# Counts of neighbours at 3.2 instead of 2.67 windows a lot, compared in pairs, and a first dense phase of three batches

## The chip, the cores and the metric

The kernel runs on one core of one Trainium2 chip. The metric is the device time of one execution in microseconds.

## The reference

Two graph layers over 6250 nodes of 256 features and 206250 edges (`src`, `dst`, sorted by `dst`; one of 8 types each), cut to what matters:

```
h  = relu(layernorm(x))
x1 = x + segment_sum(einsum('ni,roi->rno', h, weight)[edge_type, src], dst) + bias0
h  = relu(layernorm(x1))
deg = number of edges with dst n (and 1 for the node itself); dinv = 1/sqrt(deg)
out = x1 + leaky_relu(segment_sum(dinv[src]*dinv[dst] * (h @ W)[src], dst) + b, 0.2)
```

## The kernel before

Nodes are held in 50 tiles of 128. The program first normalises `x` into a table, checks the edge list and prepares keys; then `both_layers` does both layers at once. Its work is ordered by slots `n` = 0 to 578, which every engine runs through in its own loop; `Plan` computes, ahead of time, what falls into which slot.

**First layer, the lots.** Slot n below 539 has a lot: 384 edges (3 chunks of 128). POOL gathers the source rows of each chunk (L1099, 3 gathers a lot) into a ring of `RING0` = 7 lots. ScalarE makes the lot's one-hot matrices (`build_gap` L1338, three instructions, and `build_onehot` L1346), four slots ahead. TensorE sums the lot (`sum_lot`, L1599, 6 matmuls), which frees the ring's place; VectorE adds the sums to `acc` (`accumulate`, L1416), two lots at a time, since two lots share a PSUM bank and two banks are used. Every 11 lots are one tile's step: TensorE projects it with the 8 weights in two parts (`project`, L1615), VectorE and ScalarE finish and normalise it (`stage_a`, `stage_b`, `stage_c`), SyncE stores it to `table1` (L1128).

**Second layer, the counts.** The second layer is a dense product with a matrix of counts (how many edges lead from node j to node i). It is made window by window, 800 windows of 8 target nodes: VectorE compares the window's keys with node numbers (`build_hot`: L1492 for `hot_m`, 4 x 100 columns, and L1495 for `hot_lo`, 4 x 128), TensorE multiplies the two one-hots (`count`, L1629, 4 matmuls, into one of `NCOUNT` = 3 PSUM banks), ScalarE evacuates them (`evacuate`, L1275) and stores them to `counts_d`. `hots` holds `NHOT` = 8 windows; a window is counted `LEAD` = 3 slots behind its comparison. The keys of 128 windows are one set; for each of the 7 sets POOL looks up records (`look` L1080, `fetch` L1087), VectorE finds offsets and keys (`offsets` L1457 and L1459, `window_keys`), TensorE turns them (L1639), SyncE carries degrees out and in (L1196, L1203). These have slots in `Plan` that lie a fixed number ahead of the slot in which the set is first needed, `due`.

**Second layer, the dense product.** A unit is one group of 4 target tiles (13 groups) by one batch of source tiles (12 batches, `BATCHES`, mostly 5 tiles). It has two halves, each one piece in a slot: 2 matmuls of 512 columns for each source tile (`dense`, L1659; one tile of one half is called a half tile in this text). ScalarE widens the unit's counts (`widen`, L1331), SyncE loads them (`load_counts`, L1155) and the batch's features (`load_stash`, L1139), VectorE adds each piece to its sums (`add_dense`, L1523 for the first, L1525). While counting goes on, only one PSUM bank serves pieces, and there is at most one piece in two slots. First come the units of the first `EARLY_GROUPS` = 6 groups with the first `FIRST_BATCHES` = 4 batches; then SyncE moves their sums to HBM (`move_away`, L1160, 3 MB), and the other groups' units follow in the same place; when counting ends, the sums come back (`move_back`). `Plan` models TensorE's load with a pace of 3.85 us a slot and fills in pieces where there is room. A batch can't be used before its last tile is stored: batch 3 (the fourth) is there from slot 238.

The plan that results: windows in slots 13 to 312 in the rhythm 3, 3, 2, counted in slots 16 to 315; `counts_end` = 320; the move away at slot 263; 156 units, of which 1184 half tiles before lot 539 and 116 after. Half tiles per 20 slots, from slot 60 to 579: 20, 10, 0, 40, 30, 20, 45, 15, 5, 50, 35, 45, 45, 85, 80, 85, 80, 85, 80, 65, 85, 74, 65, 40, 95, 21. At the end `project1` (L1678), `close` (L1535, L1540) and POOL's addition (L1106) finish the tiles.

## Time and profile before

| | us |
|---|---|
| median of 3 runs | 2302.07 |
| lowest, highest | 2300.12, 2308.04 |
| the profiled execution, its own time | 2306.06 |
| its span, first to last instruction | 2304.3 |
| TensorE's mean granted clock | 0.953 |
| busy: TensorE, VectorE, ScalarE, POOL | 2007.3, 1219.7, 1608.9, 1643.0 |

The rows name PE for TensorE, PEld for its weight loads, DVE for VectorE, ACT for ScalarE, SP for SyncE. An idle time is put down to what ended it; "issue" means that the profile shows nothing that was waited for.

### The profile page before, as it was taken

How to read it: one execution, taken by the hardware profiler on the slowest of the kernel's cores; microseconds unless marked ns; L12 is line 12 of the kernel's file. 1: busy time of each engine (PE TensorE's matmuls, PEld its weight loads, DVE VectorE, ACT ScalarE, POOL GpSimd, SP SyncE). 2: the span in 40 equal slices, each digit the busy share in tenths (PEclk: the TensorE clock that was granted, in tenths of full speed). 3: DMA queues.
4: the chain of work that ended last, by engine and by line, in shares of the span. 5: the costliest groups of instructions: out<-in, count | busy, mean ns of one | idle time of the engine just before them, and what ended most of it. 6: DMA issues, size and time to landing. Idle time of an engine off the chain costs nothing.

```text
span 2304.3 us, 44662 instructions
## 1 busy us (share of the span) xinstructions
PE 2007.3 (87%) x14354; PEld 1797.4 (78%) x14354; DVE 1219.7 (53%) x3510; ACT 1608.9 (70%) x3919; POOL 1643.0 (71%) x1740
## 2 busy tenths in 40 slices
PE   1567788887888898879899899999999999999897
PEld 1456777776787887768788889898888898989676
DVE  7446567667568666766656633323223232334267
ACT  4646677786878888678777877776767777676440
POOL 5577777777777777777766777777777777777414
PEclk9698999999999999999989999999999999999999
DMA  9446567656766776667776777765766666666485
GB/s 289 121 123 189 177 200 225 210 186 201 244 218 222 252 232 203 187 218 241 233 246 197 238 256 243 228 194 170 222 200 190 191 196 191 183 190 162 105 225 168
DMA packets 353088, 470.37 MB, mean 204 GB/s; under 512 B 113158, under 2 KB 264886, under 8 KB 352726
## 3 DMA queue, kind: packets, MB, share of 16 engines
q0 software_dynamic: 79072, 216.18, 31.9%
q1 hardware_dynamic: 228246, 165.07, 24.5%
q10 hardware_dynamic: 45536, 86.22, 10.2%
q8 instruction: 119, 1.95, 0.4%
q14 instruction: 115, 0.94, 0.1%
HBM read 348.61 MB, written 118.71 MB: 203 GB/s over the span
## 4 chain that ended last, share of the span: by engine, by line
PE 60%; POOL 13%; issue 7%; ACT 7%; DMA 5%; DVE 4%; ACTq 1%; DVEq 0%; POOLq 0%; SPq 0%
PE ps_slot L1599 21%; PE ps_slot L1659 13%; PE ps_proj L1615 13%; POOL rows_f L1099 12%; PE ps_aux L1659 9%; DMA rows_f<-table,idxT 3%; PE ps_slot L1629 3%; ACT gap_f L1338 2%; ACT staging_f L1275 2%; ACT wide_f L1331 1%; DMA abuf_f<-counts_d 1%; DVE hots_f L1495 1%; DVE hots_f L1492 1%; ACT onehot_f L1346 1%; ACT acc_f L1261 1%
## 5 line engine op out<-in xcount | busy, mean ns | idle before, releaser
L1099 POOL DMA_INDIRECT rows_f<-table,idxT x1617 | 1538.2, 951 | 510.3 <-issue 473.8
L1599 PE MATMUL ps_slot<-onehot_f,rows_f 128*128 128x128 f32 x6468 | 870.4, 287 | 150.7 <-DMA rows_f<-table,idxT 121.8
L1599 PEld LDWEIGHTS ps_slot<-onehot_f,rows_f 128*128 128x128 f32 x6468 | 824.8, 200 | 184.3 <-DMA rows_f<-table,idxT 134.7
L1338 ACT ACTIVATE gap_f<-iota,keyT 128x128 bf16<-128x128 bf16 x1617 | 528.6, 394 | 81.1 <-ACT staging_f L1275 49.6
L1275 ACT ACTIVATE staging_f<-ps_slot 128x400 bf16<-128x400 f32 x800 | 345.8, 500 | 182.2 <-PE ps_slot L1629 179.2
L1492 DVE TENSOR_TENSOR hots_f<-ps_slot,keys_f 128x400 bf16<-128x400 bf16 x800 | 285.2, 357 | 303.5 <-PE ps_slot L1629 299.5
L1615 PE MATMUL ps_proj<-w0t,acc_f 128*128 128x256 f32 x1600 | 375.8, 389 | 0.0
L1659 PE MATMUL ps_slot<-wide_f,stash_f 128*128 128x512 f32 (+1 forms) x1410 | 345.2, 390 | 1.6 <-ACT wide_f L1331 1.5
L1346 ACT ACTIVATE onehot_f<-gap_f 128x384 f32<-128x384 bf16 x539 | 277.5, 515 | 96.6 <-PE ps_slot L1599 96.4
L1416 DVE TENSOR_TENSOR acc_f<-ps_slot,acc_f 128x256 f32 x539 | 227.2, 422 | 219.5 <-PE ps_slot L1599 151.3
L1615 PEld LDWEIGHTS ps_proj<-w0t,acc_f 128*128 128x128 f32 x1600 | 303.2, 195 | 45.4 <-issue 1.6
L1495 DVE TENSOR_TENSOR hots_f<-ps_slot,keys_f 128x512 bf16<-128x512 bf16 x800 | 329.6, 412 | 0.0
L1659 PE MATMUL ps_aux<-wide_f,stash_f 128*128 128x512 f32 x1190 | 308.4, 404 | 3.0 <-ACT wide_f L1331 3.0
L1659 PEld LDWEIGHTS ps_slot<-wide_f,stash_f 128*128 128x128 f32 x1410 | 248.0, 190 | 45.1 <-ACT wide_f L1331 2.5
L1331 ACT ACTIVATE wide_f<-abuf_f 128x512 fp32r<-128x512 bf16 (+1 forms) x404 | 217.5, 608 | 84.0 <-PE ps_slot L1659 52.0
L1629 PE MATMUL ps_slot<-hots_f 128*128 128x100 bf16 x3200 | 217.0, 211 | 60.9 <-ACT staging_f L1275 44.9
L1629 PEld LDWEIGHTS ps_slot<-hots_f 128*128 128x128 bf16 x3200 | 193.6, 115 | 87.3 <-issue 48.1
L1659 PEld LDWEIGHTS ps_aux<-wide_f,stash_f 128*128 128x128 f32 x1190 | 218.4, 193 | 44.4 <-issue 3.4
L1331 ACT ACTIVATE wide_f<-keys_f 128x512 fp32r<-128x512 bf16 (+1 forms) x215 | 117.0, 598 | 62.5 <-PE ps_slot L1659 52.9
L1525 DVE TENSOR_TENSOR sums_e_f<-ps_slot,sums_e_f 128x512 f32<-128x512 f32 x88 | 60.9, 692 | 162.7 <-PE ps_slot L1659 162.5
L1106 POOL TENSOR_TENSOR acc_f<-acc_f 128x256 f32<-128x256 f32 x50 | 36.6, 732 | 93.9 <-DVE acc_f L1540 90.9
L1261 ACT ACTIVATE acc_f<-ident 128x2048 f32<-128x2048 f32 x52 | 99.6, 1915 | 0.0
(156 smaller groups left out, 871.5 us busy)
## 6 DMA issues: line engine op xcount, KB each, us to landing
abuf_f<-counts_d SPq DMA_DIRECT2D x66, 640.0 KB
rows_f<-table,idxT POOLq DMA_INDIRECT x1617
stash_f<-table SPq DMA_DIRECT2D x15, 1280.0 KB, 7.7
keys_f<-counts_d SPq DMA_DIRECT2D x30, 640.0 KB
table<-hs_f SPq DMA_DIRECT2D x50, 256.0 KB
table<-xres SPq DMA_DIRECT2D x10, 640.0 KB, 6.7
acc_f<-x_d SPq DMA_DIRECT2D x50, 128.0 KB, 2.7
x_d<-xt_f SPq DMA_DIRECT2D x49, 128.0 KB
```

The costliest lines, as they stand in the source:

```text
L1099: eng.indirect_dma_start(rows0[:, k, c, :], None, V["table0"], bass.IndirectOffsetOnAxis(ap=idxT[:, n * LOT + c:n * LOT + c + 1], axis=0)) ...
L1275: eng.activation(staging[:, h % 2, :, (w % HSUB) * SUB:(w % HSUB + 1) * SUB], count_bank(w)[:, 0:SPAN * MW].rearrange("p (d t) -> p t d", ...
L1331: eng.activation(wide_of(i, u).rearrange("p (h c) -> p h c", c=HW), counts, ACT.Copy).then_inc(s_wide, 1)
L1338: last = eng.activation(gap[:, n % 2, c, :], iota[:, :], ACT.Abs, scale=-1.0, bias=V["key"][:, n * LOT + c:n * LOT + c + 1])
L1346: eng.activation(onehot[:, n % HOTS, :, :], gap[:, n % 2, :, :], ACT.Relu, scale=-1.0, bias=1.0).then_inc(s_oh, 1)
L1416: eng.tensor_tensor(win, part, win, ALU.add).then_inc(s_acc, 1)
L1492: eng.tensor_tensor(hot_m[:, w % NHOT, :, :].rearrange("p s (m q) -> p s m q", q=2), m_numbers.rearrange("p (m q) -> p m q", q=2).unsqueez ...
L1495: eng.tensor_tensor(hot_lo[:, w % NHOT, :, :], lo_numbers, lo_e[:, b % 2, k, :].unsqueeze(1).to_broadcast([P, P, SPAN]), ALU.is_equal).the ...
L1599: last = eng.matmul(o[:, b * W:(b + 1) * W], rows0[:, k, c, b * P:(b + 1) * P], onehot[:, n % HOTS, c, :], start=(c == 0), stop=(c == LOT ...
L1615: last = eng.matmul(ps_proj[:, 0:DF], acc[:, b * R + r, a:a + P], V["w0t"][:, r, b, :], start=False, stop=(r == R - 1 and b == NB - 1))
L1629: last = eng.matmul(o[:, j * MW:(j + 1) * MW], hot_lo[:, w % NHOT, :, j], hot_m[:, w % NHOT, j, :], start=True, stop=True)
L1659: last = eng.matmul(o, stash[:, k % 2, t, p * DF + half * P:p * DF + (half + 1) * P].bitcast(f32r), wide_of(w, u), start=(t == 0 and p == ...
```

## The change

Three things change together. `build_hots` compares two windows with one instruction of 800 and one of 1024 elements (`hot_m` and `hot_lo` of two neighbouring windows), so `s_hot` rises by one per pair, and waits until the places of both in `hots` are free. The windows are spread over 5/16 x 800 = 250 instead of 300 slots, in the rhythm 4, 4, 2, 4, 2, and the key work's distances to `due` are cut by 8 slots or 5. And `FIRST_BATCHES` is 3. The one-hots of the lots are made as before, all by ScalarE.

```diff
--- before.py
+++ after.py
@@ -16,7 +16,7 @@
 GROUP = 4
 EARLY_GROUPS = 6
 STAGED_GROUPS = 3
-FIRST_BATCHES = 4
+FIRST_BATCHES = 3
 MOVE_SLOTS = 5
 BATCH = 5
 BATCHES = (5, 5, 5, 5, 5, 5, 5, 5, 3, 2, 2, 3)
@@ -696,25 +696,26 @@
     def __init__(self, D):
         self.nlot = D.segs * LOTS
         self.tail = self.nlot + SEAM
-        last_window = D.nsub * 3 // 8
+        last_window = D.nsub * 5 // 16
         self.counts_end = FIRST_WIN + last_window + LEAD + 4
         self.win = {}
-        for w in range(D.nsub):
-            self.win.setdefault(FIRST_WIN + w * last_window // D.nsub, []).append(w)
+        assert D.nsub % 2 == 0 and NHOT % 2 == 0
+        for w in range(0, D.nsub, 2):
+            self.win.setdefault(FIRST_WIN + w * last_window // D.nsub, []).extend((w, w + 1))
         counted = [FIRST_WIN + (end * D.nw - 1) * last_window // D.nsub + LEAD + 9 for _, end in D.group]
         self.look, self.fetch, self.count_at, self.key_at, self.turn_at = {}, {}, {}, {}, {}
         self.degree_out, self.degree_in = {}, {}
         for b in range(D.sets):
             due = FIRST_WIN + b * P * last_window // D.nsub
-            self.look[due - 44 if b else 0] = b
+            self.look[due - 36 if b else 0] = b
             for i in range(len(PARTS)):
-                self.count_at[(due - 42 if b else 0) + i] = (b, i)
-            self.degree_out[due - 38 if b else 4] = b
-            self.degree_in[due - 36 if b else 6] = b
-            self.fetch[due - 30 if b else 5] = b
+                self.count_at[(due - 34 if b else 0) + i] = (b, i)
+            self.degree_out[due - 30 if b else 4] = b
+            self.degree_in[due - 28 if b else 6] = b
+            self.fetch[due - 22 if b else 5] = b
             for i in range(2):
-                self.key_at[(due - 18 if b else 8) + i] = (b, i)
-            self.turn_at[due - 14 if b else 10] = b
+                self.key_at[(due - 13 if b else 8) + i] = (b, i)
+            self.turn_at[due - 9 if b else 10] = b
         self.turn_win = {}
         for n, b in self.turn_at.items():
             self.turn_win[b] = min(w for m, ws in self.win.items() if m + LEAD > n for w in ws)
@@ -1278,7 +1279,7 @@
             def copy_keys(b):
 
                 if b >= 2:
-                    eng.wait_ge(s_hot, P * (b - 1))
+                    eng.wait_ge(s_hot, P // 2 * (b - 1))
                 eng.wait_ge(s_tp, b + 1)
                 keys, lows = (turned(b)[:, i * SPAN * P:(i + 1) * SPAN * P].rearrange("p (s w) -> p s w", s=SPAN) for i in range(2))
                 eng.activation(key_e[:, b % 2, :, :, :].rearrange("p w s q -> p s w q"),
@@ -1481,19 +1482,20 @@
                     eng.scalar_tensor_tensor(lo_w[:, :, :], hi_i[:, :, :], -float(P), rec2[:, :, :, 1], ALU.mult, ALU.add).then_inc(s_kw, 1)
                     eng.tensor_tensor(key_w[:, :, :], key_w[:, :, :], hi_i[:, :, :], ALU.add).then_inc(s_kw, 1)
 
-            def build_hot(w):
+            def build_hots(w):
 
                 b, k = divmod(w, P)
+                a = w % NHOT
                 eng.wait_ge(s_ke, 2 * (b + 1))
                 if w >= NHOT:
-                    eng.wait_ge(s_cnt, w - NHOT + 1)
+                    eng.wait_ge(s_cnt, w - NHOT + 2)
                 if w == 0:
                     eng.wait_ge(s_np, 1)
-                eng.tensor_tensor(hot_m[:, w % NHOT, :, :].rearrange("p s (m q) -> p s m q", q=2),
-                                  m_numbers.rearrange("p (m q) -> p m q", q=2).unsqueeze(1).to_broadcast([P, SPAN, MW // 2, 2]),
-                                  key_e[:, b % 2, k, :, :].unsqueeze(2).to_broadcast([P, SPAN, MW // 2, 2]), ALU.is_equal)
-                eng.tensor_tensor(hot_lo[:, w % NHOT, :, :], lo_numbers,
-                                  lo_e[:, b % 2, k, :].unsqueeze(1).to_broadcast([P, P, SPAN]), ALU.is_equal).then_inc(s_hot, 1)
+                eng.tensor_tensor(hot_m[:, a:a + 2, :, :].rearrange("p a s (m q) -> p (a s) m q", q=2),
+                                  m_numbers.rearrange("p (m q) -> p m q", q=2).unsqueeze(1).to_broadcast([P, 2 * SPAN, MW // 2, 2]),
+                                  key_e[:, b % 2, k:k + 2, :, :].rearrange("p w s q -> p (w s) q").unsqueeze(2).to_broadcast([P, 2 * SPAN, MW // 2, 2]), ALU.is_equal)
+                eng.tensor_tensor(hot_lo[:, a:a + 2, :, :], lo_numbers.unsqueeze(1).to_broadcast([P, 2, P, SPAN]),
+                                  lo_e[:, b % 2, k:k + 2, :].unsqueeze(2).to_broadcast([P, 2, P, SPAN]), ALU.is_equal).then_inc(s_hot, 1)
 
             def add_own(h):
 
@@ -1579,8 +1581,8 @@
                     offsets(*PL.count_at[n])
                 if n in PL.key_at:
                     window_keys(*PL.key_at[n])
-                for w in PL.win.get(n, ()):
-                    build_hot(w)
+                for w in PL.win.get(n, ())[::2]:
+                    build_hots(w)
                 for k in PL.fin.get(n - 1, ()):
                     close(k)
 
@@ -1619,7 +1621,7 @@
 
             def count(w):
 
-                eng.wait_ge(s_hot, w + 1)
+                eng.wait_ge(s_hot, w // 2 + 1)
                 if w >= NCOUNT:
                     eng.wait_ge(s_ev, w - NCOUNT + 1)
                 if w in turn_of:
```

The plan that results: windows compared in slots 13 to 262 and counted in slots 16 to 265; `counts_end` = 270; the first phase has 18 units instead of 24, and the move away comes at slot 210; `stash` is loaded 17 times instead of 19. Half tiles per 20 slots, from slot 60: 20, 10, 10, 35, 45, 0, 40, 35, 40, 50, 65, 85, 80, 80, 80, 85, 20, 75, 55, 10, 85, 74, 65, 40, 95, 21; 1184 before lot 539 and 116 after. Units begin at slots 183, 187, 191, 196, 200, 206, 215, 219, 223, 228, 232, 237, 242, 246, 251, 255, 259, 264 and so on.

TensorE in slots 215 to 219. L1599 is a lot, L1629 the counts (4 matmuls a window), L1615 a projection. Before:

```order
L1599 MATMUL ps_slot<-onehot_f,rows_f 128x128 x6
L1629 MATMUL ps_slot<-hots_f 128x100 x12
L1599 MATMUL ps_slot<-onehot_f,rows_f 128x128 x6
L1615 MATMUL ps_proj<-w0t,acc_f 128x256 x8
L1629 MATMUL ps_slot<-hots_f 128x100 x8
L1599 MATMUL ps_slot<-onehot_f,rows_f 128x128 x6
L1629 MATMUL ps_slot<-hots_f 128x100 x12
L1599 MATMUL ps_slot<-onehot_f,rows_f 128x128 x6
L1629 MATMUL ps_slot<-hots_f 128x100 x12
L1599 MATMUL ps_slot<-onehot_f,rows_f 128x128 x6
L1629 MATMUL ps_slot<-hots_f 128x100 x8
```

The same slots in the changed kernel, where the lines are L1601, L1631, L1617, and L1661 is a dense piece:

```order
L1601 MATMUL ps_slot<-onehot_f,rows_f 128x128 x6
L1631 MATMUL ps_slot<-hots_f 128x100 x8
L1661 MATMUL ps_aux<-wide_f,stash_f 128x512 x10
L1601 MATMUL ps_slot<-onehot_f,rows_f 128x128 x6
L1617 MATMUL ps_proj<-w0t,acc_f 128x256 x8
L1631 MATMUL ps_slot<-hots_f 128x100 x16
L1601 MATMUL ps_slot<-onehot_f,rows_f 128x128 x6
L1631 MATMUL ps_slot<-hots_f 128x100 x16
L1661 MATMUL ps_aux<-wide_f,stash_f 128x512 x10
L1601 MATMUL ps_slot<-onehot_f,rows_f 128x128 x6
L1631 MATMUL ps_slot<-hots_f 128x100 x8
L1601 MATMUL ps_slot<-onehot_f,rows_f 128x128 x6
```

The counts of a slot went from 8 or 12 matmuls to 8 or 16, and a dense piece stands in every second slot where there was none.

VectorE about slot 219 to 220, before: an addition of a lot to `acc`, the last stage of a tile (L1442), `own` (L1504) and the comparisons of four windows.

```order
L1416 ISA
L1416 TENSOR_TENSOR acc_f<-ps_slot,acc_f 128x16x16
L1442 TENSOR_TENSOR hs_f<-hs_f 128x256
L1504 TENSOR_TENSOR own_f<-staging_f,identb 128x64
L1492 TENSOR_TENSOR hots_f<-ps_slot,keys_f 128x400
L1495 TENSOR_TENSOR hots_f<-ps_slot,keys_f 128x512
L1492 TENSOR_TENSOR hots_f<-ps_slot,keys_f 128x400
L1495 TENSOR_TENSOR hots_f<-ps_slot,keys_f 128x512
L1492 TENSOR_TENSOR hots_f<-ps_slot,keys_f 128x400
L1495 TENSOR_TENSOR hots_f<-ps_slot,keys_f 128x512
L1492 TENSOR_TENSOR hots_f<-ps_slot,keys_f 128x400
L1495 TENSOR_TENSOR hots_f<-ps_slot,keys_f 128x512
```

In the changed kernel, with a burst of key offsets (L1458, L1460), the lines L1494 and L1497 comparing pairs:

```order
L1460 TENSOR_REDUCE n_less_f<-keys_f 128x1
L1458 TENSOR_SCALAR keys_f<-recs_f,startp 128x512
L1460 TENSOR_REDUCE n_less_f<-keys_f 128x1
L1494 TENSOR_TENSOR hots_f<-ps_slot,keys_f 128x800
L1497 TENSOR_TENSOR hots_f<-ps_slot,keys_f 128x1024
L1494 TENSOR_TENSOR hots_f<-ps_slot,keys_f 128x800
L1497 TENSOR_TENSOR hots_f<-ps_slot,keys_f 128x1024
L1396 TENSOR_LOAD offr
L1417 ISA
L1417 TENSOR_TENSOR acc_f<-ps_slot,acc_f 128x16x16
L1417 ISA
```

Four windows took eight comparisons, of 400 and 512 columns; four now take four, of 800 and 1024. The offsets of set 6, which came at slots 259 to 262, now stand here.

## Rows read from the trace of the kernel before

**Rows 1.** The page, busy us of each engine, share of the span, instructions.

```profile
PE 2007.3 (87%) x14354; PEld 1797.4 (78%) x14354; DVE 1219.7 (53%) x3510; ACT 1608.9 (70%) x3919; POOL 1643.0 (71%) x1740
```

**Rows 2.** Line L1099, the gathers: durations ns, first and last start; POOL's idle time before them.

```profile
L1099 POOL DMA_INDIRECT rows_f<-table,idxT x1617: 942/949/1781, 75.8 to 2165.8; - x180
...
  issue: 473.8, 1554
  PE ps_slot L1599: 36.5, 63
```

**Rows 3.** Waits of POOL from 1120 to 1350 us: total us, times, longest.

```profile
POOL rows_f L1099 <- PE ps_slot L1599: 20.1, 10, 4.7
```

**Rows 4.** Gathers (L1099) by stretch: us, POOL busy (count), clock, DMA share, GB/s.

```profile
70.00:810.00 740.00, 533.36 (x560) 0.92 0.63 197
70.00:1170.00 1100.00, 796.93 (x836) 0.93 0.65 205
70.00:1340.00 1270.00, 912.64 (x958) 0.93 0.66 207
1410.00:1820.00 410.00, 310.30 (x328) 1.00 0.68 199
```

**Rows 5.** Additions to acc (L1416) by stretch, VectorE busy (count).

```profile
70.00:810.00 740.00, 76.29 (x182) 0.92 0.63 197
70.00:1170.00 1100.00, 113.12 (x270) 0.93 0.65 205
70.00:1340.00 1270.00, 130.72 (x312) 0.93 0.66 207
810.00:920.00 110.00, 12.13 (x29) 0.97 0.68 214
```

**Rows 6.** All engines by stretch: PE, PEld, DVE, ACT, POOL busy (count).

```profile
1170.00:1340.00 170.00, 155.04 (x1236) 139.31 (x1235) 107.25 (x338) 136.54 (x337) 115.72 (x123) 0.96 0.70 223
1410.00:1820.00 410.00, 410.00 (x2509) 366.70 (x2508) 123.78 (x296) 295.49 (x700) 310.30 (x328) 1.00 0.68 199
```

**Rows 7.** Waits from 1170 to 1340 us.

```profile
DVE hots_f L1492 <- PE ps_slot L1629: 42.4, 19, 5.6
...
ACT staging_f L1275 <- PE ps_slot L1629: 20.9, 16, 3.2
...
PE ps_slot L1629 <- ACT staging_f L1275: 10.7, 6, 3.8
```

**Rows 8.** Timeline of TensorE: start us, us, instruction (a lot's 6 matmuls appear as 12).

```profile
1104.32 0.70 PE L1629 MATMUL ps_slot<-hots_f 128*128 128x100 bf16 x12
1104.86 1.57 PE L1599 MATMUL ps_slot<-onehot_f,rows_f 128*128 128x128 f32 x12
```

**Rows 9.** Timeline of VectorE, comparisons.

```profile
1199.43 0.35 DVE L1492 TENSOR_TENSOR hots_f<-ps_slot,keys_f 128x400 bf16<-128x400 bf16 x1
1199.70 0.41 DVE L1495 TENSOR_TENSOR hots_f<-ps_slot,keys_f 128x512 bf16<-128x512 bf16 x1
1200.03 0.35 DVE L1492 TENSOR_TENSOR hots_f<-ps_slot,keys_f 128x400 bf16<-128x400 bf16 x1
```

**Rows 10.** The page, evacuation of counts: busy us, mean ns, idle before.

```profile
L1275 ACT ACTIVATE staging_f<-ps_slot 128x400 bf16<-128x400 f32 x800 | 345.8, 500 | 182.2 <-PE ps_slot L1629 179.2
```

**Rows 11.** Timeline of VectorE and TensorE behind a burst of key offsets.

```profile
1129.71 0.41 DVE L1416 TENSOR_TENSOR acc_f<-ps_slot,acc_f 128x256 f32 x1
...
1130.91 0.55 PE L1599 MATMUL ps_slot<-onehot_f,rows_f 128*128 128x128 f32 x1 [6.34 <-DVE acc_f L1416]
```

**Rows 12.** The page, fp32 additions from PSUM, 256 and 512 columns: busy us, mean ns.

```profile
L1416 DVE TENSOR_TENSOR acc_f<-ps_slot,acc_f 128x256 f32 x539 | 227.2, 422 | 219.5 <-PE ps_slot L1599 151.3
...
L1525 DVE TENSOR_TENSOR sums_e_f<-ps_slot,sums_e_f 128x512 f32<-128x512 f32 x88 | 60.9, 692 | 162.7 <-PE ps_slot L1659 162.5
```

**Rows 13.** Waits of the whole span before counting matmuls.

```profile
PE ps_slot L1629 <- ACT staging_f L1275: 44.9, 37, 4.1
...
PEld ps_slot L1629 <- DVE hots_f L1495: 25.5, 34, 2.7
```

## Prediction

> **What bounds the kernel now.** I read the page's busy shares first, then the gathers' own line, then the stretches. TensorE is busy for 87% of the span and POOL for 71% [rows 1], which points to TensorE, but the gathers say otherwise: a gather occupies POOL for 0.949 us and the next begins 0.305 us later (473.8 us of "issue" gaps over 1554 times), a step of 1.254 us. There are 1617 gathers and 35 look-ups of the same length, and 1652 x 1.254 = 2072 us; they run from 75.8 to 2166.8 us, 2091 us [rows 2]. So for 91% of the span the kernel goes at the pace at which POOL can issue: 3 gathers, 3.76 us a lot. POOL lost only 2091 - 2072 = 19 us to anything else. The line lists 63 waits for TensorE's L1599, 36.5 us; 10 of them, 20.1 us, lie between 1120 and 1350 us [rows 3], and the other 53 average 0.31 us, the ordinary gap. Taking the ordinary gap off, the stall in that one stretch is 20.1 - 3 = **17 us**, and it is all that a change of TensorE's, VectorE's or ScalarE's work before lot 539 can win.
>
> Why it is there: the ring holds 7 lots. The gathers issued up to a time, divided by 3, less the lots added to `acc` by then, are the lead of POOL in lots (those landed and summed but not yet added included). Up to 810 us it is 560/3 - 182 = 4.7. By 1170 us it is 836/3 - 270 = 8.7, and by 1340 us 958/3 - 312 = 7.3, with POOL waiting in between: the ring is full [rows 4, 5]. From 1170 to 1340 us, 42 lots take 170 us, 4.05 us each; TensorE is busy 155.0 us of them (3.69 a lot), ScalarE 136.5 (3.25), VectorE 107.3 (2.55) [rows 5, 6]. These are lots 270 to 311, where counting (2.67 windows a lot) and the dense pieces of phase two run together. Afterwards TensorE is busy 410 us of 410, but POOL issues 328 gathers in them, 411 us' worth: TensorE just keeps up [rows 4, 6]. Behind the last gather come 137 us of tail.
>
> **The change, part by part.**
>
> *Two windows per comparison.* The comparison of 400 elements begins 0.27 us before that of 512, which begins 0.33 us before the next: 0.60 us a window [rows 9]. 112 more elements cost about 0.055 us, 0.49 ns each, which leaves some 0.075 us per instruction. A pair then costs 800 x 0.49 + 0.075 = 0.47 and 1024 x 0.49 + 0.075 = 0.58 us, 1.05 against 1.20: over 400 pairs VectorE has about 60 us less to do. It is not the last to arrive in the full stretch (it waits 42.4 us for TensorE's counts in 170 us [rows 7]), so I cost this at nothing; were VectorE full, 3.2 x 0.075 = 0.24 us a lot would come back. Per lot VectorE's comparisons go from 2.67 x 0.60 = 1.60 to 3.2 x 0.525 = 1.68 us.
> The 400 elements come from PSUM and go through in 0.27 us, 1.5 elements a nanosecond. The Trainium skill (VectorE: DVE Perf Modes, the perf-mode tier table) gives two-tensor operations with any PSUM operand one element per cycle at 0.96 GHz. This trace speaks against that; by that rule a pair would be near 2 us, and that is a rival below.
>
> *3.2 windows a lot.* TensorE: three windows take 1104.86 - 1104.32 = 0.54 us, 0.18 each; 0.53 more a lot is **0.10 us a lot** [rows 8]. ScalarE: an evacuation keeps it busy 345.8/800 = 0.43 us, so 0.23 us a lot more, 3.25 to 3.48 of 3.76 us [rows 6, 10]. The slots now hold 4, 4, 2, 4, 2 windows, before 3, 3, 2. There are three count banks, so a fourth window in a slot must wait until the first has been evacuated: one evacuation lasts 0.50 us [rows 10], TensorE is there 0.54 us after it began the first, so the wait is at least some 0.2 us when ScalarE is prompt. When it isn't, the nearest rows are the waits that exist: 10.7 us in 6 times, 1.8 us each [rows 7]. Three slots in five: between 0.12 and 1.1 us a lot. I take 0.2, near the lower end, because ScalarE itself stood waiting for counts 16 times in these 42 lots [rows 7], so it is often there first.
> Eight windows of one-hots are kept. Before, 8 windows were exactly three slots' work, so VectorE, building for slot n, needed the counts of TensorE's slot n. 3.2 x 3 is 9.6, so now it needs part of slot n + 1, and what stands behind the comparison on VectorE (the additions of the lots, the addition of a dense piece, both with TensorE waiting for them) comes up to a slot later. Bound from below nothing (TensorE has a slot in between); from above the one case in the trace: VectorE's burst of key offsets, at the end of which TensorE had stood 6.34 us for L1416 [rows 11]. Six such bursts remain; I take nothing for those before lot 183, where POOL's lead is short and covers them, and 0.1 us a lot in the full stretch for this.
>
> *Counting ends at lot 267 instead of 317; phase one is 3 batches (18 units), moved away at slot 210 instead of 263.* Dense work before lot 539 and after it is unchanged (1184 and 116 half tiles), and from slot 458 on both plans are the same, so **the tail costs the same**. Gathers and look-ups keep their number; on POOL look-ups 1 to 6 move to earlier lots. SyncE issues the 3 MB moves earlier and two `stash` loads fewer. What changes is where the dense work lies. While counting goes on, the old plan has pieces of 240 half tiles in slots 180 to 320, with nearly nothing between 206 and 238. The new one has them from 183 to 210 and without a break from 215 to the end of counting (the order of TensorE in slots 215 to 219, shown above, is where it begins; 11 units of 5 halves x 2 in 52 slots, 2.2 half tiles a lot; the old full stretch: 10 units in slots 268 to 311, 2.3). So the mixture that filled the ring for 42 lots now comes for 52, with denser counts, and it comes straight after 27 lots of the same kind.
>
> **The sum.** Full stretch: 4.05 (as now) + 0.10 (counts) + 0.2 (fourth window) + 0.1 (VectorE later) = 4.45; less 0.1 since the clock in my reference was 0.96 and the burst of offsets no longer coincides with the move: **4.35 us a lot** against POOL's 3.76. 52 lots x 0.59 = 31 us. Lots 183 to 210 now run at 110/29 = 3.79 [rows 5, 6]; with 0.3 more, 27 x 0.33 = 9 us of lead are used. The lead at 810 us, 4.7 lots, leaves 8.7 - 4.7 = 4 lots or 15 us to fill, and slots 210 to 215 give back 3 us: 15 - 9 + 3 = 9, of which I count 7, since the lead wanders by a lot. Stall 31 - 7 = 24 us, and 1 us for going into the dense stretch, where TensorE has no spare, with a full ring. Gone is the old stall of 17. Net 24 + 1 - 17 = **+8 us**: 2306.06 becomes 2314 for the profiled run, and, as that run lies 4 us above the median of the runs, 2302.07 becomes **2310 us**. Ends: with 4.1 us a lot the stall is 18 - 9 = 9 us, net -8; with 4.65 it is 46 - 7 = 39 and up to 5 us more later, net +27.
>
> **The rivals.**
> *The stall goes (faster).* The old stall began when a burst of key offsets on VectorE, the move of 3 MB and the first load of counts behind it fell into slots 259 to 268; TensorE stood 6.34 us at its start [rows 11], and the lead went from short to full within 120 us. Now the move (210) and the burst (219 to 222) are nine slots apart and VectorE has spare time. If TensorE then holds 3.9 us a lot, 52 x 0.14 = 7 us fit into the lead and the stall is gone: 2302 - 17 = 2285; half gone, 2293. It decides at about 4.2 us a lot (52 x 0.44 = 23, less 9, is 14: a gain of 3). Against it: from 1170 to 1340 us, long after the burst, the pace stayed at 4.05.
> *Nothing changes.* The stall moves 50 lots earlier with its size: 2302, within 7 us. A measurement of this kernel can tell about 0.3%, 7 us, from no change.
> *Paired comparisons fall to one element a cycle.* The fp32 additions from PSUM go one by one: 512 elements take 0.27 us more than 256, 1.05 ns each [rows 12]. If the pair's shapes lose the rate that the 400-element rows show and fall to this one, a pair takes 1824 x 1.05 = 1.92 us and twice 0.075, 2.07; 1.6 pairs a lot are 3.3 us, and VectorE's other work in the full stretch is 2.55 - 1.60 = 0.95: 4.25 us a lot through all 250 lots of counting, 0.49 x 250 = 120 us less the lead: about 2410. The tier table of the Trainium skill (VectorE: DVE Perf Modes) would have it so. The rows for 400 elements, with the same operand in PSUM, do not [rows 9].
> *A pair comes too late.* A count now waits for both windows' comparisons. TensorE's weight loads waited for L1495 34 times [rows 13]; at 0.5 us more each, 17 us over 250 lots, of which a third falls where it counts: +5 us on the forecast's side. The Trainium skill (Perfetto Trace Analysis, Optimizing Scalar/DVE Operations) advises breaking instructions up where an engine that isn't full makes others wait, which speaks against pairing.
>
> **How the numbers follow.** Forecast, stall larger (late pairs included): 0.50, of which 0.11 within 0.3%. Nothing changes: 0.15, with 0.01 to either side. Stall mostly or wholly gone: 0.32, of which 0.29 over 0.3%. One element a cycle: 0.03. Together faster 0.30, same 0.27, slower 0.43. The range takes in half to nearly all of the gain and the upper end of the sum: 2288 to 2330.
>
> **What would show it.** In the profile after: POOL's waits for L1599 over 0.5 us at about lots 220 to 270 (900 to 1100 us), 24 us of them; a pace of 4.35 us a lot there; L1494 and L1497 at a step of 0.47 and 0.58 us; TensorE's L1631 waiting for ScalarE far more often than the 37 times of now [rows 13]; the last gather at about 2175 us and again 137 us behind it. I am wrong if POOL's waits for TensorE fall below 17 us in all, or if the last gather comes before 2160 us, or if the tail changes by more than 3 us.

## The result, and the profile after

| | before | after |
|---|---|---|
| median, us (4 runs of each, on one chip) | 2301.10 | 2455.95 |
| lowest, highest | 2299.66, 2308.04 | 2452.55, 2463.31 |
| profiled execution: own time, span | 2306.06, 2304.3 | 2452.55, 2450.3 |
| TensorE's mean granted clock | 0.953 | 0.940 |

The ratio is 1.0671, with a 95% interval from 1.0652 to 1.069: slower by 155 us where 8 were forecast, and far above the range. The direction was right, the size was not.

The page of the kernel after, busy us of each engine, beside [rows 1]; then the gathers, the evacuations and the two paired comparisons (busy, mean ns | idle before them):

```profile
PE 2037.2 (83%) x14354; PEld 1823.9 (74%) x14354; DVE 1171.3 (48%) x2710; ACT 1615.8 (66%) x3919; POOL 1639.0 (67%) x1740
...
L1100 POOL DMA_INDIRECT rows_f<-table,idxT x1617 | 1533.8, 949 | 658.9 <-issue 454.0
...
L1276 ACT ACTIVATE staging_f<-ps_slot 128x400 bf16<-128x400 f32 x800 | 340.1, 502 | 206.5 <-PE ps_slot L1631 201.7
...
L1494 DVE TENSOR_TENSOR hots_f<-ps_slot,keys_f 128x800 bf16<-128x800 bf16 x400 | 228.0, 570 | 388.7 <-PE ps_slot L1631 387.5
...
L1497 DVE TENSOR_TENSOR hots_f<-ps_slot,keys_f 128x1024 bf16<-128x1024 bf16 x400 | 271.8, 680 | 0.0
```

Hardly any engine has more to do: POOL 4 us less, VectorE 48 less, ScalarE 7 more, and TensorE 30 more, at a mean granted clock of 0.940 instead of 0.953. All shares have fallen. So the 146 us by which the span grew are, nearly all, waiting. The gathers tell whose. The same line by itself: durations, first and last start, POOL's idle time before them:

```profile
L1100 POOL DMA_INDIRECT rows_f<-table,idxT x1617: 940/946/1265, 75.4 to 2309.4; - x180
...
  issue: 454.0, 1490
  PE ps_slot L1601: 204.9, 127
```

The last gather starts at 2309.4 instead of 2165.8 us [rows 2]: 143.6 us later; behind it come 140.9 us instead of 138.5. POOL waited 204.9 us for TensorE's lot sums instead of 36.5, and its ordinary gaps shrank by 19.8: 148.6 us more of standing, the whole loss. When? Gathers and additions by stretch, beside [rows 4, 5] (us, POOL or VectorE busy with them (count), clock, DMA share, GB/s):

```profile
70.00:400.00 330.00, 232.68 (x245) 0.85 0.57 177
70.00:810.00 740.00, 489.66 (x516) 0.90 0.60 187
70.00:1170.00 1100.00, 706.16 (x744) 0.91 0.61 193
70.00:1340.00 1270.00, 805.26 (x849) 0.91 0.62 196
```

```profile
70.00:400.00 330.00, 31.16 (x74) 0.85 0.57 177
70.00:810.00 740.00, 68.95 (x164) 0.90 0.60 187
70.00:1170.00 1100.00, 100.41 (x239) 0.91 0.61 193
70.00:1340.00 1270.00, 115.58 (x275) 0.91 0.62 196
```

At 400 us POOL's lead, reckoned as in the prediction, is 245/3 - 74 = 7.7 lots: the ring is full before lot 80. (Before, at that time, 77 lots had been added and 244 gathers issued: 4.3.) From 400 to 810 us a lot then takes 410/(164 - 74) = 4.6 us, from 810 to 1170 us 4.8; by 1340 us 275 lots are done where 312 were, 37 lots, or 139 us at 3.76. So the loss does not sit in the 52 lots for which it was forecast; it runs through all of counting. By 810 us, before lot 164 was added, POOL had issued 516 gathers where it had issued 560, 44 x 1.254 = 55 us' worth; by 1340 us 849 instead of 958, 137 us' worth.

What the engines waited for from 400 to 1300 us, after:

```profile
DVE hots_f L1494 <- PE ps_slot L1631: 307.7, 145, 7.9
POOL rows_f L1100 <- PE ps_slot L1601: 186.4, 92, 6.1
ACT staging_f L1276 <- PE ps_slot L1631: 161.9, 67, 7.0
PE ps_slot L1631 <- ACT staging_f L1276: 158.2, 118, 5.2
```

and before, in the same 900 us:

```profile
DVE hots_f L1492 <- PE ps_slot L1629: 215.8, 76, 11.4
...
ACT staging_f L1275 <- PE ps_slot L1629: 115.2, 69, 9.2
...
PE ps_slot L1629 <- ACT staging_f L1275: 37.3, 29, 4.1
...
POOL rows_f L1099 <- PE ps_slot L1599: 23.5, 29, 4.7
```

TensorE waits for ScalarE, ScalarE waits for TensorE, VectorE waits for TensorE, each longer than before, and each engine is less busy in the stretch than it was (TensorE 712.7 us instead of 777.6, VectorE 536.7 instead of 592.0, ScalarE 645.3 instead of 699.8, POOL 561.3 instead of 670.7). A fifth wait has grown too, that of TensorE's weight loads for the comparisons; whole span of after, against 25.5 us in 34 times [rows 13]:

```profile
PEld ps_slot L1631 <- DVE hots_f L1497: 78.5, 50, 5.3
```

It overlaps with the wait for evacuations. Of TensorE's 205.7 us before counts over the whole span, 68.6 us (44 times) are cases in which the weight load of the same matmul had first waited for a comparison; the evacuation came last in them, mostly 0.4 to 1.0 us behind the comparison. So not all of the 205.7 us is the bank's alone. One of the longest waits (their mean is 1.3 us, the longest 5.2), in the timeline of after (start us, us, instruction, idle before it and what ended it):

```profile
1040.23 1.15 ACT L1332 ACTIVATE wide_f<-abuf_f 128x512 fp32r<-128x512 bf16 x2 [0.97 <-DMA abuf_f<-counts_d]
...
1041.29 1.65 ACT L1332 ACTIVATE wide_f<-abuf_f 128x512 fp32r<-128x512 bf16 x3
...
1042.85 0.97 ACT L1339 ACTIVATE gap_f<-iota,keyT 128x128 bf16<-128x128 bf16 x3
...
1043.72 0.51 ACT L1347 ACTIVATE onehot_f<-gap_f 128x384 f32<-128x384 bf16 x1
1044.13 1.66 ACT L1276 ACTIVATE staging_f<-ps_slot 128x400 bf16<-128x400 f32 x4
...
1044.76 0.49 PE L1631 MATMUL ps_slot<-hots_f 128*128 128x100 bf16 x4 [5.01 <-ACT staging_f L1276]
...
1045.36 0.57 DVE L1494 TENSOR_TENSOR hots_f<-ps_slot,keys_f 128x800 bf16<-128x800 bf16 x1 [4.72 <-PE ps_slot L1631]
...
1048.22 0.94 POOL L1100 DMA_INDIRECT rows_f<-table,idxT  x1 [3.84 <-PE ps_slot L1601]
```

It is a slot of four windows. TensorE has counted three, and its fourth (4 matmuls) needs the bank of the first. ScalarE, at the end of its slot before, waits 0.97 us for counts from HBM and widens five tiles; then it makes a lot's one-hots, and only at 1044.13 does it evacuate. TensorE stands 5.01 us at the fourth window, with its lot sum queued behind; VectorE stands 4.72 us for the places, and POOL 3.84 us for the ring. With three windows in a slot and three banks, each window needs only evacuations of the slot before, and TensorE need not meet ScalarE inside the slot.

### The profile page after: what moved, and what is told of

Read it like the earlier page. It is cut to its first block, busy times and chain, and to the rows that moved or that the text cites. A ratio compares the mean times of both kernels' runs of the same rounds, so it can differ in the third digit from the quotient of the medians.

```text
span 2450.3 us, 43462 instructions
## 1 busy us (share of the span) xinstructions
PE 2037.2 (83%) x14354; PEld 1823.9 (74%) x14354; DVE 1171.3 (48%) x2710; ACT 1615.8 (66%) x3919; POOL 1639.0 (67%) x1740
## 4 chain that ended last, share of the span: by engine, by line
PE 52%; ACT 16%; POOL 11%; issue 7%; DVE 5%; DMA 4%; ACTq 2%; SPq 0%; DVEq 0%; POOLq 0%
PE ps_slot L1601 17%; PE ps_proj L1617 11%; POOL rows_f L1100 11%; PE ps_slot L1661 10%; PE ps_aux L1661 8%; ACT staging_f L1276 5%; ACT gap_f L1339 4%; PE ps_slot L1631 3%; ACT wide_f L1332 2%; ACT onehot_f L1347 2%; DMA rows_f<-table,idxT 1%; DVE hots_f L1497 1%; PE ps_slot L1680 1%; DMA abuf_f<-counts_d 1%; ACT acc_f L1262 1%
## 5 line engine op out<-in xcount | busy, mean ns | idle before, releaser
L1601 PE MATMUL ps_slot<-onehot_f,rows_f 128*128 128x128 f32 x6468 | 885.4, 291 | 107.2 <-DMA rows_f<-table,idxT 83.0
L1601 PEld LDWEIGHTS ps_slot<-onehot_f,rows_f 128*128 128x128 f32 x6468 | 841.0, 204 | 142.4 <-DMA rows_f<-table,idxT 94.6
L1631 PE MATMUL ps_slot<-hots_f 128*128 128x100 bf16 x3200 | 229.6, 215 | 222.0 <-ACT staging_f L1276 205.7
L1494 DVE TENSOR_TENSOR hots_f<-ps_slot,keys_f 128x800 bf16<-128x800 bf16 x400 | 228.0, 570 | 388.7 <-PE ps_slot L1631 387.5
L1631 PEld LDWEIGHTS ps_slot<-hots_f 128*128 128x128 bf16 x3200 | 200.2, 116 | 250.8 <-issue 163.5
L1617 PE MATMUL ps_proj<-w0t,acc_f 128*128 128x256 f32 x1600 | 372.0, 386 | 0.0
L1661 PE MATMUL ps_slot<-wide_f,stash_f 128*128 128x512 f32 (+1 forms) x1490 | 365.0, 390 | 7.2 <-ACT wide_f L1332 7.2
L1617 PEld LDWEIGHTS ps_proj<-w0t,acc_f 128*128 128x128 f32 x1600 | 300.5, 193 | 44.0 <-issue 0.9
L1661 PEld LDWEIGHTS ps_slot<-wide_f,stash_f 128*128 128x128 f32 x1490 | 263.3, 190 | 53.5 <-ACT wide_f L1332 4.4
L1661 PE MATMUL ps_aux<-wide_f,stash_f 128*128 128x512 f32 (+1 forms) x1110 | 299.3, 417 | 0.8 <-DVE sums_e_f L1525 0.6
L1497 DVE TENSOR_TENSOR hots_f<-ps_slot,keys_f 128x1024 bf16<-128x1024 bf16 x400 | 271.8, 680 | 0.0
L1661 PEld LDWEIGHTS ps_aux<-wide_f,stash_f 128*128 128x128 f32 x1110 | 211.4, 201 | 41.5 <-DVE sums_e_f L1525 0.8
```

The source lines that it names most:

```text
L1494: eng.tensor_tensor(hot_m[:, a:a + 2, :, :].rearrange("p a s (m q) -> p (a s) m q", q=2), m_numbers.rearrange("p (m q) -> p m q", q=2).uns ...
L1497: eng.tensor_tensor(hot_lo[:, a:a + 2, :, :], lo_numbers.unsqueeze(1).to_broadcast([P, 2, P, SPAN]), lo_e[:, b % 2, k:k + 2, :].unsqueeze( ...
L1601: last = eng.matmul(o[:, b * W:(b + 1) * W], rows0[:, k, c, b * P:(b + 1) * P], onehot[:, n % HOTS, c, :], start=(c == 0), stop=(c == LOT ...
L1617: last = eng.matmul(ps_proj[:, 0:DF], acc[:, b * R + r, a:a + P], V["w0t"][:, r, b, :], start=False, stop=(r == R - 1 and b == NB - 1))
L1631: last = eng.matmul(o[:, j * MW:(j + 1) * MW], hot_lo[:, w % NHOT, :, j], hot_m[:, w % NHOT, j, :], start=True, stop=True)
L1661: last = eng.matmul(o, stash[:, k % 2, t, p * DF + half * P:p * DF + (half + 1) * P].bitcast(f32r), wide_of(w, u), start=(t == 0 and p == ...
```

## The experiments

The theories of the expectations: BANKS, the slots of four windows meet three count banks, so TensorE and ScalarE must meet inside every such slot. PLACES, 8 places of one-hots against 3 slots' work of 9.6 windows, so VectorE needs the counts of a later slot of TensorE's. DENSITY, there is simply more work a lot. PHASE, the first dense phase of three batches. Expectations given in us were written for a chip on which the kernel before takes 2301 us. The edits shown are cut to their main lines. A ratio is the time over that of the kernel before on the same chip; the numbers in brackets are its 95% interval.

### On two chips where the kernel before takes 2770 us

The first three sets of runs ran on two chips on which the kernel before itself takes 2745 to 2773 us. POOL does not set the pace there: in a kernel that is nearly the one before (`phase3` below) the gathers last as long as elsewhere, but POOL waits for TensorE 296 us, and TensorE's loads before counts stand for no visible reason. The waits of `phase3`, whole span (`remote`: the profile names no instruction as what ended the wait; such rows stand in none of the profiles from chips of the usual time):

```profile
POOL rows_f L1099 <- PE ps_slot L1599: 296.0, 135, 6.8
POOL rows_f L1099 <- remote: 291.0, 167, 3.0
...
PEld ps_slot L1629 <- issue: 261.1, 249, 5.4
```

The ratios from there rank the parts; their sizes are taken from the later sets.

**phase3**: the kernel before with `FIRST_BATCHES = 3` and nothing else.

```diff
-FIRST_BATCHES = 4
+FIRST_BATCHES = 3
```

> The kernel before with FIRST_BATCHES = 3 alone (windows one at a time, 2.67 a lot). Theory BANKS (a slot with four windows has TensorE's fourth count wait for ScalarE's evacuation of the first, since there are three count banks): no slot has four windows, so the time stays at 2302 within 10 us. Theory PLACES (VectorE needs counts of one slot later, since 9.6 windows ahead do not fit into 8 places of one-hots): also 2302. Theory DENSITY (3.2 windows a lot are too many for ScalarE and TensorE together): also 2302. Theory PHASE (the dense work laid into the counting by the first phase of three batches costs it): most of the loss of 155 us is here, over 2400.

Measured: 2790.96 us against 2770.16, 1.007 [1.0049, 1.0091]. A small loss, a little over the 10 us that three of the theories allowed; PHASE, which put most of the loss here, is out.

**pairs**: the change with 2.67 windows a lot, four batches and the key work's old distances (these not in the lines shown); only the pairing is left. The rhythm becomes 4, 2, 2, so it has slots of four as well.

```diff
-        last_window = D.nsub * 5 // 16
+        last_window = D.nsub * 3 // 8
-FIRST_BATCHES = 3
+FIRST_BATCHES = 4
```

> The kernel before with paired comparisons alone (2.67 windows a lot, so slots hold 4, 2, 2 windows; four batches). BANKS: one slot in three has four windows against three in five of the change, over 300 instead of 250 lots: about two thirds of the loss at most, 2360 to 2405, with TensorE's waits for L1276 of 90 us or more. PLACES: a pair needs the count of seven windows back, so part of the slots wait for a slot later: 2330 to 2370. DENSITY and PHASE: 2302 within 10 us.

Measured: 2829.31, 1.0202 [1.0161, 1.0243]. A loss where DENSITY and PHASE expected none; as a ratio it is below what BANKS gave (1.026 to 1.045) and within PLACES (1.012 to 1.03).

**singles**: the change with `build_hot` of the kernel before, one window at a time (3.2 windows a lot, rhythm 4, 3, 3, 3, 3).

```diff
-                for w in PL.win.get(n, ())[::2]:
-                    build_hots(w)
+                for w in PL.win.get(n, ()):
+                    build_hot(w)
```

> The changed kernel with one window per comparison again (3.2 a lot, slots of 3, 3, 3, 3, 4; three batches). BANKS: one slot in five has four windows, over 250 lots: 2320 to 2360. PLACES: eight places against 9.6 windows ahead as in the change: 2420 or more. DENSITY and PHASE: 2430 to 2460, as the change.

Measured: 2857.91, 1.0318 [1.0271, 1.0364]. Density, phase and the new key distances together cost more than the pairing. The ratio lies above BANKS (1.025 at most) and below PLACES and DENSITY (1.05 or more).

**smooth**: the change, compared in pairs, but counted and evacuated in the rhythm of single windows. The last line's replacement stands in six more places, among them the evacuations and `Plan`'s model of the load.

```diff
+        self.cwin = {}
+        for w in range(D.nsub):
+            self.cwin.setdefault(FIRST_WIN + w * last_window // D.nsub, []).append(w)
-                for w in PL.win.get(n - LEAD, ()):
+                for w in PL.cwin.get(n - LEAD, ()):
```

> The changed kernel, paired comparisons kept as they are, but TensorE, ScalarE and the addition of the own windows go by the rhythm 3, 3, 3, 3, 4 instead of 4, 4, 2, 4, 2. BANKS: 2320 to 2370, TensorE's waits for L1276 down from 206 us to under 90. PLACES, DENSITY, PHASE: 2430 to 2460.

Measured: 2855.87, 1.0297 [1.0259, 1.0335]. BANKS expected 1.03 at most where the whole change costs 1.067; what this took off is read against the next run.

**after_again**: the change itself, for a measure on such a chip.

> The changed kernel itself, unchanged, as the yardstick of the chip on which this set runs: 1.067 of before where before takes about 2301 us. On a chip where before takes 2770 us, as in the set with phase3, pairs, singles and smooth, all theories expect about 1.03 to 1.05, since there before is no longer at POOL's pace.

Measured: 2877.73 against 2772.9, 1.0375 [1.0346, 1.0404]; POOL waits 459.7 us for TensorE. The change loses 105 us here; that it is less than 155 because POOL was already waiting in the kernel before is likely, but no run shows it. TensorE's waits for evacuations, in `after_again`, in `smooth` and in `phase3`:

```profile
PE ps_slot L1631 <- ACT staging_f L1276: 182.5, 111, 7.0
```

```profile
PE ps_slot L1634 <- ACT staging_f L1279: 114.0, 71, 7.1
```

```profile
PE ps_slot L1629 <- ACT staging_f L1275: 108.8, 73, 3.7
```

The smooth rhythm brings this wait nearly down to that of `phase3` (and misses the 90 us expected), and yet gives back only 22 of the 105 us (the two runs are from two chips; one slot in five still holds four windows). So here the slots of four are the smaller part of the loss, against BANKS. `smooth` was not run on a chip of the usual time.

**lead2**: the change with windows counted two slots behind their comparison; 6.4 windows are then ahead, and the 8 places suffice.

```diff
-LEAD = 3
+LEAD = 2
```

> The changed kernel with LEAD = 2: a window is counted two slots behind its comparison instead of three, so 6.4 windows ahead fit into the 8 places of one-hots. PLACES: the loss mostly goes, 1.00 to 1.02 of before. BANKS: slots of four windows remain, so it stays at the changed kernel's ratio within 0.01. DENSITY: also stays.

Measured: 2865.88, 1.0329 [1.0307, 1.0351], 12 us less than `after_again`. PLACES expected the loss mostly gone, and is wrong in that form.

**smooth_lead2**: both edits together.

> The changed kernel with LEAD = 2 and the counts' rhythm 3, 3, 3, 3, 4 (comparisons in pairs as in the change). PLACES: as lead2, 1.00 to 1.02. BANKS: as smooth, half or more of the loss gone. If both causes act together this is the only one that reaches before's time or goes below it. DENSITY: the changed kernel's ratio.

Measured: 2849.29, 1.0279 [1.0262, 1.0297]: 28 us of the 105 are back, less than 22 + 12 us, what the two edits give back one by one, and far from the half or more that BANKS and PLACES expected.

**density4**: `singles` with `FIRST_BATCHES = 4`.

> The kernel before with 3.2 windows a lot and the key distances of the change, but one window per comparison and four batches in the first phase: density alone, slots of 3, 3, 3, 3, 4. Where before takes about 2301 us: DENSITY says most of the 155 us, 2400 or more; BANKS 2310 to 2350; PLACES 2400 or more (9.6 windows ahead against 8 places). Where before takes 2770 us: singles was 1.032 and phase3 1.007 of before, so 1.02 to 1.03.

Measured: 2827.12 against 2745.19, 1.0302 [1.0268, 1.0337]. Against the 1.0318 of `singles` the phase makes no difference that these runs can tell. Density and the new key distances by themselves cost more than the pairing (1.0202 [1.0161, 1.0243]).

**early**: the change with ScalarE's evacuations ahead of the lots' one-hots in its slot. The widening of the slot before still stands ahead of them.

```diff
-                if n + AHEAD < PL.nlot:
-                    if n + AHEAD + 1 < PL.nlot:
-                        build_gap(n + AHEAD + 1)
-                    build_onehot(n + AHEAD)
                 for w in PL.win.get(n - LEAD, ()):
                     evacuate(w)
+                if n + AHEAD < PL.nlot:
+                    if n + AHEAD + 1 < PL.nlot:
+                        build_gap(n + AHEAD + 1)
+                    build_onehot(n + AHEAD)
```

> The changed kernel with ScalarE's evacuations at the beginning of its slot, ahead of the one-hots of the lot four slots on. BANKS (TensorE's fourth count waits for ScalarE, which is held up by its one-hots and widenings): the waits for L1276 shrink and 15 to 60 us come back. PLACES: VectorE's waits are for TensorE's counts, little changes, within 10 us of the changed kernel. On a chip where before takes 2770 us the same signs, with sizes of a half.

Measured: 2826.28, 1.029 [1.0249, 1.033], against the change's 1.0375. A ScalarE that is sooner at the bank gives back about a fifth of the loss (24 us, each against the kernel before in its own set), as BANKS expected; TensorE's waits for evacuations are 159.3 us, against 182.5.

### The count banks, on a chip of the usual time (before: 2302.35 us)

**banks4**: the change with a fourth count bank. The bank comes from the table of node numbers, which the comparisons then read from SBUF instead of PSUM (`lo_numbers` likewise; the code that filled the bank goes). So two things change at once.

```diff
-NCOUNT = 3
+NCOUNT = 4
-        m_numbers = numbers[:, SPAN * P:SPAN * P + MW]
+        m_numbers = iota_m[:, :]
```

> The changed kernel with four count banks instead of three: the node numbers are read from SBUF (iota4, iota_m), which frees their PSUM bank. BANKS, sharper now: with four windows in a slot and three banks TensorE and ScalarE must meet inside every such slot, so each slot costs the longer of the two instead of the mean; a fourth bank gives back a slot of slack. Then most of the loss against before goes: under 1.02 where before takes 2301 us, and from 1.0375 to 1.02 or less where before takes 2770 us; TensorE's waits for L1276 fall to half of 182 us or less. PLACES: no change, within 0.005 of the changed kernel. DENSITY: no change either.

Measured: 2391.14, 1.0386 [1.0366, 1.0406], against the change's 1.0671. BANKS expected under 1.02, PLACES and DENSITY no change: all three miss.

**before_banks4**: the same edit to the kernel before.

> The kernel before with the fourth count bank. BANKS: it has at most three windows a slot, so little: 0.985 to 1.0 of before; TensorE's waits for L1275 fall. PLACES and DENSITY: 1.0.

Measured: 2334.61, 1.0143 [1.0127, 1.016].

**sbuf3**: the kernel before with the numbers in SBUF and three banks, so the edit's side effect alone.

> The kernel before with the node numbers read from SBUF and three banks, the control for the two others: what the operand's place costs by itself. If nothing, 1.0 within 0.003 of before and comparisons of 0.36 and 0.41 us as now; if two SBUF operands get in POOL's way, gathers longer than 0.95 us and a slower kernel.

Measured: 2329.99, 1.0129 [1.011, 1.0148]. So the fourth bank does nothing for the kernel before that these runs can tell (2334.61 against 2329.99), where BANKS expected 0.985 to 1.0, and the numbers in SBUF cost it 28 us. The gathers of the page of `sbuf3`, and below of `banks4`, show where: they last 973 and 993 ns in the mean, instead of 951 and 949.

```profile
L1099 POOL DMA_INDIRECT rows_f<-table,idxT x1617 | 1573.0, 973 | 492.7 <-issue 476.8
```

```profile
L1100 POOL DMA_INDIRECT rows_f<-table,idxT x1617 | 1605.5, 993 | 522.3 <-issue 474.7
```

For the change the bank does much. TensorE's waits of `banks4`, whole span (L1597 is the lot sum there, L1627 the counts):

```profile
PE ps_slot L1597 <- DMA rows_f<-table,idxT: 136.5, 63, 9.3
PE ps_slot L1597 <- DVE acc_f L1415: 64.7, 27, 7.5
PE ps_slot L1627 <- ACT staging_f L1276: 55.8, 33, 9.0
...
PEld ps_slot L1627 <- DVE hots_f L1493: 21.9, 23, 1.9
```

The wait for evacuations falls from 205.7 to 55.8 us (under half of it, as BANKS expected), the loads' wait for comparisons from 78.5 to 21.9, POOL's for TensorE from 204.9 to 47.6, and the time by 65 us although each gather is 44 ns longer (1617 x 0.044 = 71 us of POOL's time). That 65 us is what was measured, bank and slower gathers together. Set against `sbuf3`, the kernel before with its numbers in SBUF, the change with four banks is 2.6% slower instead of 6.7%, 61 us instead of 155, so by this estimate some 94 us hang on the missing bank. It is an estimate: the change with its numbers in SBUF and three banks was not run, and a slower POOL also hides some waits. What has grown in the same rows is TensorE's wait for VectorE's additions, 64.7 us where the change has 24.0; its first row, the wait for gathers, is 83.0 in the change and 121.8 in the kernel before.

### The parts again, on a chip of the usual time (before: 2302.79 us)

**phase3_b**, **pairs_b** and **singles_b** are the kernels `phase3`, `pairs` and `singles`.

> The kernel of run phase3 again, for such a chip. BANKS, PLACES, DENSITY: 1.00 within 0.004. PHASE: 1.01 or more.

> The kernel of run pairs again, for such a chip (2.67 a lot in slots of 4, 2, 2, four batches). BANKS: 100 slots of four against 150 in the change, 1.02 to 1.045 of before. DENSITY: 1.00. PLACES: 1.00 to 1.02.

> The kernel of run singles again, for a chip where before takes about 2301 us (3.2 windows a lot one by one, slots of 3, 3, 3, 3, 4, three batches). BANKS: 1.005 to 1.025 of before, POOL's waits for TensorE under 80 us. PLACES or DENSITY as the main cause: 1.05 or more.

Measured: `phase3_b` 2316.60, 1.006 [1.004, 1.008]; `pairs_b` 2364.31, 1.026 [1.0229, 1.0292]; `singles_b` 2407.04, 1.0455 [1.043, 1.0481]. In us: 14, 61 and 104 (density, phase and new key distances together, so density with the distances about 90). 61 + 104 = 165, near the 155 of the whole: the parts nearly add up. The new key distances were never run by themselves; what they cost is not known. By their expectations `pairs_b` fits BANKS (1.02 to 1.045) and lies above PLACES (1.02 at most) and DENSITY (none); `singles_b` lies above BANKS (1.025) and below PLACES and DENSITY (1.05 or more), with POOL's waits for TensorE at 146.4 us where BANKS had under 80; `phase3_b` lies between the 1.004 and the 1.01 of the theories. Pairing alone, with less work for VectorE and no more windows a lot, costs 61 us. TensorE's waits in `pairs_b`:

```profile
PE ps_slot L1631 <- ACT staging_f L1276: 163.0, 102, 6.7
PE ps_slot L1601 <- DMA rows_f<-table,idxT: 75.5, 39, 7.1
...
PEld ps_slot L1631 <- DVE hots_f L1497: 74.1, 38, 2.5
```

163.0 us for evacuations, against 44.9 [rows 13], with the same count of windows and evacuations of the same 500 ns: what is new is that half of the windows come four to a slot. A pair also waits for the places of both its windows, and a count for the comparison of both: 74.1 us of the loads' waits, against 25.5 [rows 13], partly under the same 163.0. How the 61 us divide between these, no run shows. And a us of such waits is not a us of time: they rose by 118 us here, the time by 61, while TensorE's waits for gathers fell from 121.8 to 75.5.

**three**: 3.0 windows a lot, three in all but two of 266 slots, single comparisons, four batches, and the change's key distances (not in the lines shown). Two slots of four are left of the 150 of the change.

```diff
-        last_window = D.nsub * 3 // 8
+        last_window = D.nsub // 3
```

> The kernel before with 266 slots of counting, 3.0 windows a lot one by one, three in nearly every slot, four batches and the key distances of the change. BANKS: no slot of four, so no loss: 0.995 to 1.005 of before. DENSITY: a third to two thirds of the loss of 3.2, 1.02 or more. PLACES: nine windows ahead against eight places, 1.02 or more.

Measured: 2363.57, 1.0259 [1.0239, 1.0279]. BANKS in its narrow form, that slots of four are all of it, expected next to no loss here, and is wrong: 61 us are lost almost without them. DENSITY and PLACES both expected 1.02 or more; the run does not part them, nor the key distances from either. TensorE's waits:

```profile
PE ps_slot L1600 <- DMA rows_f<-table,idxT: 88.5, 51, 7.1
PE ps_slot L1600 <- DVE acc_f L1417: 66.6, 29, 9.7
PE ps_slot L1630 <- ACT staging_f L1276: 52.2, 39, 3.9
```

The evacuations are as before (52.2 against 44.9). The additions are not: 66.6 us against 26.6.

### The places, on another such chip (before: 2304.23 us)

**three_lead2**: `three` with `LEAD = 2`.

> This is the kernel three (3.0 windows a lot, three in every slot, single comparisons, four batches) with LEAD = 2: a window is counted two slots behind its comparison, so 6 windows are ahead of their counts and the 8 places of one-hots no longer make VectorE wait for a later slot of TensorE's. PLACES: the coupling of VectorE and TensorE through the 8 places was what made three slower; the ratio falls from 1.026 to 1.012 or less, and TensorE's waits for the additions (66.6 us) fall below 35 us. RENDEZVOUS through the count banks or plain density: the places matter little; the ratio stays at 1.020 to 1.030, and TensorE waits for the one-hots of the comparison more often instead.

Measured: 2333.58, 1.013 [1.0113, 1.0147], half of the loss of `three`. RENDEZVOUS (the meeting at the count banks in general, or plain density) expected 1.02 to 1.03, and does not explain this half. TensorE's waits now:

```profile
PE ps_slot L1600 <- DMA rows_f<-table,idxT: 122.0, 56, 7.2
PE ps_slot L1630 <- ACT staging_f L1276: 47.6, 39, 4.4
...
PE ps_slot L1600 <- DVE acc_f L1417: 14.6, 8, 4.8
```

The wait for the additions falls from 66.6 to 14.6 us. As PLACES has it: with 9 windows ahead and 8 places, VectorE stood before a comparison with the additions queued behind it. 1.013 is a hair above what PLACES put as its limit; the other half of the loss stays. The kernel before was not run with `LEAD = 2`, and 14.6 us is also less than its own 26.6, so a part of the gain may be one that it would have had too.

**lead2_b**: the change with `LEAD = 2`.

> The change with LEAD = 2 alone; on the chips on which before takes 2770 us it took 0.5 % off (1.0375 to 1.0329). PLACES as a main cause: on a chip of the usual time the ratio falls from 1.067 to 1.050 or less and POOL's waits for TensorE from 205 to under 150 us. BANKS as the main cause (as the fourth bank's 1.0386 has it): 1.055 to 1.067, since the three count banks stay, with TensorE's waits for ScalarE's evacuations at 150 to 210 us as in the change.

Measured: 2416.45, 1.0483 [1.0449, 1.0518], 43 us less than the change's 155. Its rows:

```profile
PE ps_slot L1631 <- ACT staging_f L1276: 181.4, 156, 4.3
```

The ratio is as PLACES expected and below what BANKS did (1.055 or more); POOL's waits for TensorE, 157.3 us, miss PLACES' 150 by little, and the waits for evacuations stay, as BANKS expected. So both couplings act. The bank's part is the larger on these chips, 65 us as measured and some 94 by the estimate; the places' is 43. Bank and `LEAD = 2` were not tried together, so that these parts add is not shown, and where the nearest thing was tried, in `smooth_lead2` on the slower chips, 22 and 12 us gave 28. What the rest is, the mere work of DENSITY or the key distances, stays open. No run beat the kernel before.

## Why the prediction was wrong

*What bounds the kernel.* Right, and still so in the stretch after counting: the loss is POOL's standing, to within the 2.4 us of the tail.

*Pairing costs nothing.* Half right. The prices hold: in the timeline of VectorE after, paired comparisons that follow one another start 0.48 and 0.60 us apart, where 0.47 and 0.58 stood.

```profile
1058.43 0.68 DVE L1497 TENSOR_TENSOR hots_f<-ps_slot,keys_f 128x1024 bf16<-128x1024 bf16 x1
1059.03 0.56 DVE L1494 TENSOR_TENSOR hots_f<-ps_slot,keys_f 128x800 bf16<-128x800 bf16 x1
1059.51 0.68 DVE L1497 TENSOR_TENSOR hots_f<-ps_slot,keys_f 128x1024 bf16<-128x1024 bf16 x1
```

So the rival of one element a cycle is out. The trace disagrees, for these shapes, with the tier that the perf-mode tier table of the Trainium skill (VectorE: DVE Perf Modes) gives to an operand in PSUM. VectorE is busy 48 us less. But the step looked only at VectorE's time and at late pairs. That pairs must be scheduled in pairs, which turns 3, 3, 2 into 4, 2, 2 or 4, 4, 2, 4, 2, was seen only as part of the density; alone it costs 61 us (`pairs_b`), and taken out of the change it returns 49 (2455.95 - 2407.04, on two chips of the usual time).

*The fourth window.* This is the step that failed. It named the mechanism, and gave "between 0.12 and 1.1 us a lot. I take 0.2, near the lower end, because ScalarE itself stood waiting for counts 16 times in these 42 lots". TensorE's waits for evacuations rose by 205.7 - 44.9 = 161 us over 250 lots, 0.64 us a lot, three times the 0.2 and the middle of the bounds, and they did so over all of counting, not over the 52 lots in which the term was charged. A fourth bank took 150 us of these waits away, and 65 us or more of the time. The reason was a bad one: that ScalarE often waits for TensorE says nothing against TensorE waiting for ScalarE at other times. When two engines must meet in each slot, both waits grow together, and in the rows above both did. That a slot then costs whichever of the two is the longer in it is the likely reading; no run measures it.

*VectorE one slot later.* Taken as 0.1 us a lot in the full stretch; 43 us over 250 lots are 0.17, in all of counting (`lead2_b`). The sign by which it was to act, TensorE waiting for the additions, is not in the change itself (24.0 us against 26.6); it shows where the bank or the slots of four are out of the way (64.7 in `banks4`, 66.6 in `three`). In the change the 8 places show as VectorE's waits for counts: 387.5 us, and 222.5 in `lead2_b`.

*A pair comes too late.* The rival had the loads' waits for comparisons grow by 17 us and the time by 5. They grew by 53 (78.5 against 25.5), to near the 70.5 of `singles_b`, which has no pairs; they fell to 21.9 with the fourth bank. So in the change they come more from the density and the meeting at the banks than from the pairs; in `pairs_b` the pairs alone bring them to 74.1.

*Only in the full stretch.* "I take nothing for those before lot 183, where POOL's lead is short and covers them." The same thought stood behind pricing the fourth window and the late VectorE for lots 183 to 267 alone, and this made the error large. The spare lead was 8.7 - 4.7 = 4 lots, 15 us, once. At 0.6 to 1 us a lot it is gone within 25 lots, and from there each lot pays: the kernel before ran its early lots at 3.9 us (from 400 to 810 us), next to POOL's pace. The lead was in fact full at 400 us, and 55 of POOL's 137 us were lost before lot 164, where the forecast had nothing. With 0.64 + 0.17 us for 250 lots and the lead of 15 us, the two terms alone would have come to 250 x 0.81 - 15 = 188 us: too much, since a us of TensorE's wait costs less than a us, but of the right order where 8 was forecast. (A slip without weight: 11 units of 5 halves x 2 in 52 slots are 2.1 half tiles a lot, not 2.2.)

*The first phase.* Its stall was to move and not to grow; alone it costs 14 us (`phase3_b`), within the range of that term. *The tail* was to stay the same within 3 us: it did (2.4).

*What was to show it.* L1631 waiting for ScalarE "far more often than the 37 times": 153 times. POOL's waits at lots 220 to 270, 24 us: 59.0 us at lots 224 to 275 (1100 to 1340 us), and 204.9 in all. The pace there, 4.35 us a lot: 240/51 = 4.7. Last gather at 2175: 2309.4.
